# A graph network kernel: SyncE gathers ten blocks of layer two row by row, in place of GpSimd

## The reference

```python
def _sage_conv(x, src, dst, W_l, b_l, W_r):
    msgs = x[src]
    agg = jax.ops.segment_sum(msgs, dst, num_segments=N_NODES)
    deg = jax.ops.segment_sum(jnp.ones((src.shape[0],), x.dtype), dst, num_segments=N_NODES)
    mean = agg / jnp.maximum(deg, 1.0)[:, None]
    return mean @ W_l + b_l + x @ W_r
...
h = jax.nn.relu(_sage_conv(x, src, dst, W1_l, b1, W1_r))
h = jax.nn.relu(_sage_conv(h, src, dst, W2_l, b2, W2_r))
return h @ W3 + b3
...
x = _layernorm(x + _L0_gnn_ref(x, edge_index, ...), axis=-1)
```

## Time and profile before

| | us |
|---|---|
| median of 3 runs (lowest, highest) | 3304.33 (3302.39, 3308.82) |
| the profiled execution | 3299.5 |
| its span, first to last instruction | 3297.4 |
| PE busy, of the span | 2754.1 |
| POOL busy | 2379.8 |
| DVE busy | 1457.7 |
| ACT busy | 497.5 |

### The profile page before, as it was taken

One profiled execution on the slowest core, in us unless ns is written; L12 is line 12 of the kernel. 1 busy time (PEld: TensorE's weight loads), 2 busy tenths in 40 slices (PEclk: granted clock), 3 DMA queues, 4 the chain that ended last, 5 costly groups with the idle time before them and its releaser, 6 DMA issues.

```text
span 3297.4 us, 61445 instructions
## 1 busy us (share of the span) xinstructions
PE 2754.1 (84%) x13183; PEld 2294.5 (70%) x13184; DVE 1457.7 (44%) x3301; ACT 497.5 (15%) x1511; POOL 2379.8 (72%) x2439
## 2 busy tenths in 40 slices
PE   4788899899899899888866779878879879988876
PEld 3555687678678688677754567767768767767765
DVE  5676555555555555433323333333333333333332
ACT  2000110101111111111110112112112112212113
POOL 4765777677677677767747777777777777777775
PEclk7989999999999999999988889999999999999999
DMA  4443577577677777877655657757757757757743
GB/s 117 130 134 112 169 237 246 173 231 238 203 219 238 222 218 240 263 217 218 206 180 177 190 174 224 216 172 227 216 162 233 221 169 225 225 168 229 219 128 109
DMA packets 495816, 650.77 MB, mean 197 GB/s; under 512 B 184192, under 2 KB 414454, under 8 KB 492503
## 3 DMA queue, kind: packets, MB, share of 16 engines
q0 software_dynamic: 116736, 318.92, 32.6%
q1 hardware_dynamic: 298164, 253.95, 25.2%
q10 hardware_dynamic: 80800, 76.82, 7.7%
HBM read 579.07 MB, written 70.40 MB: 197 GB/s over the span
## 4 chain that ended last, share of the span: by engine, by line
PE 29%; POOL 24%; issue 18%; DVEq 14%; DMA 7%; DVE 7%; SPq 1%; ACT 1%; ACTq 0%; POOLq 0%; PEld 0%; PEldq 0%
POOL ring L420 24%; PE ps L507 16%; PE ps L578 5%; DMA ring<-z_rows,scol 4%; PE psY L622 3%; DVEq L917 2%; DVE oh L971 2%; PE psY L611 2%; DVEq L937 2%; DVE acc L907 1%; DMA counts<-scratch 1%; DVE oh L929 1%; PE psB L552 1%; DVEq L1067 1%; DVEq L914 1%
## 5 line engine op out<-in xcount | busy, mean ns | idle before, releaser
L507 PE MATMUL ps<-ring,oh 128*125 128x257 f32 (+1 forms) x6384 | 1586.9, 400 | 375.7 <-DMA ring<-z_rows,scol 203.6
L507 PEld LDWEIGHTS ps<-ring,oh 128*125 128x125 f32 x6384 | 1221.7, 196 | 649.5 <-issue 462.4
L420 POOL DMA_INDIRECT ring<-in_x,scol x1216 | 1193.4, 981 | 493.7 <-issue 349.8
L420 POOL DMA_INDIRECT ring<-z_rows,scol x1216 | 1185.8, 975 | 397.7 <-issue 355.5
L929 DVE SCALAR_TENSOR_TENSOR oh<-dcol,cf,iota 128x500 f32<-128x500 int16 x798 | 591.4, 741 | 609.9 <-issue 328.3
L907 DVE TENSOR_TENSOR acc<-ps,acc x802 | 338.8, 422 | 608.0 <-PE ps L507 415.4
L578 PE MATMUL ps<-scratch 128*125 128x257 f32 (+1 forms) x2000 | 481.2, 388 | 19.4 <-issue 13.4
L578 PEld LDWEIGHTS ps<-scratch 128*125 128x125 f32 x2000 | 456.1, 294 | 39.3 <-issue 21.5
L1268 ACT ACTIVATE work<-psT,b2c 128x125 f32<-128x125 f32 x200 | 62.0, 362 | 1196.2 <-PE psT L673 1196.2
L1232 ACT COPY work<-psY 125x256 f32<-125x256 f32 x100 | 37.2, 372 | 1306.1 <-PE psY L611 1306.1
L552 PE MATMUL psB<-oh 128*128 (+1 forms) x546 | 160.2, 391 | 81.7 <-DVE oh L971 80.7
(11 more groups left out here) (120 smaller groups left out, 1100.2 us busy)
## 6 DMA issues: line engine op xcount, KB each, us to landing
scratch<-counts SPq DMA_DIRECT2D x200, 312.5 KB
scratch<-in_x SPq DMA_DIRECT2D x114, 512.0 KB, 4.2
scratch<-z_rows SPq DMA_DIRECT2D x114, 512.0 KB, 4.0
counts<-scratch SPq DMA_DIRECT2D x25, 1250.0 KB
work<-in_x ACTq DMA_DIRECT2D x200, 125.0 KB
ring<-in_x,scol POOLq DMA_INDIRECT x1216
ring<-z_rows,scol POOLq DMA_INDIRECT x1216
scratch<-in_x SPq DMA_DIRECT2D x114, 128.0 KB, 5.2
```

What stands on the lines that cost most here:

```text
L420: pool.indirect_dma_start(ring[:, slot, b, 0:D], None, rows_dram, bass.IndirectOffsetOnAxis(scol[:, n - C0:n - C0 + 1], 0)).then_inc(rows[ ...
L507: mm = pe.matmul(psA[0:WN, bass.ds(bank, W)], oh[:, R if later else slot, b, :], ring[:, slot, b, 0:W], start=(b == 0), stop=(b == nb - 1))
```

## The change

In layer two, and there alone, two groups of each of the five stages get their first block from SyncE: the groups 27 and 47 of the stage (`own_group`), both in slot 3, behind the tenth and the twentieth dense step. The block lands in a place of its own behind the ring, `own`. GpSimd leaves out the first block of these ten groups (`lead`), so that it issues 1206 blocks in layer two where it issued 1216.

- SyncE loads the block's 128 addresses, straight from the input `src`, into one partition of `tables` (`load_picks`, two small DMAs for each stage). In the dense steps 2 to 9 and 11 to 18 of a stage, behind the three DMAs of `load_step`, it reads 16 of the addresses into registers (two loads of eight) and issues 16 DMAs of one row of 1 KB, whose source address is in a register (`own_rows`). That makes 128 DMAs for a block and 1280 in all. Before the second block's first rows it waits until TensorE has read the first one.
- In steps 9 and 19 SyncE waits until all 128 rows have landed and group 23 or 43 of the stage has been read, and then adds one to a new semaphore, `s_led` (`own_ready`).
- TensorE, ahead of the fourth group of each dense round in layer two, computes in registers whether this is an own group (`lead_row`), waits for `s_led` and takes the first block's operand from an address in a register. For the fourth slot it counts its semaphore in a register of its own, `turn3`, since only three blocks come from GpSimd there; this adds one register instruction to each round of layer one and to the other rounds of layer two.
- Some small tiles change their place, to make room.

```diff
+LEAD = (R - 1) * GB * RW
+def own_group(l, w, k):
+    return (40 if l else 4 + STAGE) + STAGE * w + 8 + 20 * k + 19
...
+            def own_rows(rows_dram, l, w, t):
+                m = w
+                k, s = (0, t - 2) if t < 10 else (1, t - 11)
+                if not 0 <= s < 8:
+                    return
+                if s == 0 and k == 0:
+                    sp.wait_ge(s_picks[m % 2], 32 * (m // 2 + 1))
+                if s == 0 and k == 1:
+                    sp.wait_ge(s_gr[l], own_group(l, w, 0) + 1)
+                elif s == 0 and w > 0:
+                    sp.wait_ge(s_gr[l], own_group(l, w - 1, 1) + 1)
+                for e in range(s * 16, s * 16 + 16, 8):
+                    sp.load(pick, picks[:, m % 2, k, e:e + 8])
+                    for j in range(8):
+                        sp.dma_start(own[e + j:e + j + 1, 0:D],
+                                     rows_dram[bass.ds(sp.snap(pick[j], min_val=0, max_val=N - 1), 1), :]).then_inc(
+                                         s_own[k], 16)
+            def own_ready(l, w, t):
+                if t not in (9, STEPS - 1):
+                    return
+                k = t // 10
+                sp.wait_ge(s_own[k], 16 * P * (w + 1))
+                sp.wait_ge(s_gr[l], own_group(l, w, k) - R + 1)
+                sp.sem_inc(s_led, 1)
...
                 for t in range(STEPS):
                     load_step(z_dram, w, t)
+                    if t == 2 and w + 1 < HW:
+                        load_picks(1, w + 1)
+                    own_rows(z_dram, 1, w, t)
+                    own_ready(1, w, t)
...
-                    for b in range(GB):
-                        if g >= R and b == 0:
+                    lead = int(l == 1 and g in own_groups(l))
+                    for b in range(lead, GB):
+                        if g >= R and b == lead:
                             pool.wait_ge(s_gr[l], g - R + 1)
...
+                    row = ring[:, slot, b, 0:W]
+                    if l == 1 and slot == R - 1 and b == 0:
+                        row = rows_flat[:, bass.ds(pe.snap(lead, min_val=LEAD, max_val=R * GB * RW), W)]
...
-                pe.wait_ge(rows[l][i], pe.snap(turn, min_val=16, max_val=16 * GB * NGG))
+                pe.wait_ge(rows[l][i], pe.snap(turn3 if i == R - 1 else turn, min_val=16, max_val=16 * GB * NGG))
...
+                def lead_row(j):
+                    pe.reg_alu(body, j, 205, ALU.mult)
...
+                    pe.reg_add(turn3, turn3, 48)
+                    pe.wait_ge(s_led, pe.snap(led, min_val=1, max_val=2 * HW + 1))
+                    pe.reg_alu(lead, lead, R * GB * RW - LEAD, ALU.mult)
+                    pe.reg_add(lead, lead, LEAD)
...
+                        if l == 1 and dense and i == R - 1:
+                            lead_row(j)
+                        elif i == R - 1:
+                            pe.reg_add(turn3, turn3, 16 * GB)
```

More of the change, by code:

```diff
@@ L78, in hot_end, with own_groups @@
     return 4 + STAGE * (w + 1) + STAGE
+LEAD = (R - 1) * GB * RW
+def own_group(l, w, k):
+    return (40 if l else 4 + STAGE) + STAGE * w + 8 + 20 * k + 19
+def own_groups(l):
+    return [own_group(l, w, k) for w in range(HW) for k in range(2)]
 def window_order():
@@ L156, in build @@
         acc = sb("acc", [P, (NW + 1) * RW])
-        ring = sb("ring", [P, R, GB, RW])
+        rows_all = sb("ring", [P, R * GB + 1, RW])
+        ring = rows_all[:, 0:R * GB, :].rearrange("p (r b) n -> p r b n", b=GB)
+        rows_flat = rows_all.rearrange("p q n -> p (q n)")
+        own = rows_all[:, R * GB, :]
         scol = sb("scol", [P, NC], I32)
@@ L230, in build @@
         k_i = k_u.bitcast(I32)
+        one = scratch[0:1, u:u + P]
+        u += P
         assert u <= 2 * JP * PW + 2 * SJ * (WN + RW)
@@ L251, in build @@
         rows = [[sem(f"rows{l}_{k}") for k in range(R)] for l in range(2)]
+        s_own = [sem(f"s_own{k}") for k in range(2)]
+        s_led = sem("s_led")
+        s_picks = [sem(f"s_picks{k}") for k in range(2)]
         s_oh = [sem(f"s_oh{l}") for l in range(2)]
@@ L392, in _ @@
                 sp.wait_ge(s_zd[q], 16 * (NW // 2))
+            give(sp, s_led)
+            load_picks(1, 0)
             fallback(z_dram, 0, STEPS)
@@ L401, in _ @@
             pool.memset(ed_i[:, 1, NT - 1, :], int(BIG)).then_inc(s_pad, 1)
-            pool.memset(ring[:, :, :, D:RW], 1.0).then_inc(s_ring1, 1)
+            pool.memset(rows_all[:, :, D:RW], 1.0).then_inc(s_ring1, 1)
             ready = 0
@@ L506, in pair @@
                 for b in range(nb):
+                    row = ring[:, slot, b, 0:W]
+                    if l == 1 and slot == R - 1 and b == 0:
+                        row = rows_flat[:, bass.ds(pe.snap(lead, min_val=LEAD, max_val=R * GB * RW), W)]
                     mm = pe.matmul(psA[0:WN, bass.ds(bank, W)], oh[:, R if later else slot, b, :],
-                                   ring[:, slot, b, 0:W], start=(b == 0), stop=(b == nb - 1))
+                                   row, start=(b == 0), stop=(b == nb - 1))
                     if b == nb - 2 and not later:
@@ L714, in four @@
                             fallback(l, general.index(i) % 2)
+                    if l == 1 and dense:
+                        pe.reg_mov(lead, LEAD)
                 if l == 0:
                     for i in range(4):
+                        if i == R - 1:
+                            pe.reg_add(turn3, turn3, 16 * GB)
                         one_group(i)
@@ L728, in layer @@
                             four(builds=True)
[L729 to L730 removed]
+                        with pe.Fori(0, STEPS // 2) as j:
+                            four(builds=True, dense=True, j=j)
                     with pe.Fori(0, 2):
                         four(general=(0, 1, 2, 3))
[L733 to L734 removed]
+                    with pe.Fori(0, STEPS // 2) as j:
+                        four(dense=True, j=j)
                 else:
@@ L740, in layer @@
                             four()
-                        with pe.Fori(0, STEPS // 2):
-                            four(dense=True)
+                        with pe.Fori(0, STEPS // 2) as j:
+                            four(dense=True, j=j)
                 with pe.Fori(0, STEPS // 4 + (1 if l else -2)):
```

35 lines of the change are left out of this document (26 added, 9 removed).

## The result

| | before | after |
|---|---|---|
| median of 7 runs (lowest, highest), us | 3303.17 (3299.98, 3308.82) | 3286.62 (3281.95, 3294.27) |
| ratio to before, 95% interval | | 0.9953 [0.9939, 0.9967] |
| the profiled execution, its span | 3299.5, 3297.4 | 3292.56, 3290.7 |
| layer one, GpSimd's first to last gather | 1679.7 | 1686.3 |
| layer two, GpSimd's first to last gather | 1556.0 | 1540.4 |

The change makes the kernel 0.47% faster, 15.5 us by the ratio. By the interval of the ratio the gain is anything from 10.9 to 20.1 us, so the size of the miss is read better from the length of layer two than from the medians.

The account below looks back on a forecast made before the run. GpSimd's issue of 1216 blocks was taken to bound layer two. Span 3297.4 - 12.5 (ten blocks) + 1.5 (layer one) = 3286.4 us; against the median 3304.3 - 11.0 = 3293.3 us, range 3288 to 3307.

Parts of the forecast that it names:

- The bound: Layer two: lasts exactly as long as GpSimd needs for its 1216 blocks, 1556 us, at 1.28 us each.
- The worth of a block: GpSimd, layer two: each block left out saves 1.25 to 1.28 us; ten blocks, 12.5 us taken.
- at most the mean: GpSimd, layer two: upper end of a block's worth, 1556/1216 = 1.28 us, as slow blocks may go on being slow.
- Layer one's 1.5 us: TensorE, layer one: one more register instruction in each of 76 rounds costs 1.5 us, bounds 0 and 3.2.
- SyncE's rows: SyncE's queue, layer two: 0.38 us a row, 8.8 us of a 10.2 us step; upper end 0.65 and 13.1 us.
- SyncE keeps up: SyncE's queue, dense steps with rows: at the lower end 8.8 us of issue fits in a step of 10.2 us.
- rival one: SyncE can't issue the rows in time and GpSimd stalls: about 3405 us at 0.7 us a row; chance 0.11.
- The wait for `s_led`: TensorE, tightest in stage 3 at step 9: the block is complete with 3 us to spare; price 0.
- TensorE's seven instructions: TensorE, before each fourth group in layer two's 50 dense rounds: 15 to 35 us, hidden beside waiting for rows; price 0.
- the ring's reserve: GpSimd's 16-block ring, layer two: TensorE may be late by an estimated 8 us before GpSimd stalls.
- Rival three: Layer two: one-row DMAs crowd one DMA engine; about 3420 us at 0.3 us a row; chance 0.07.

Follow-up runs that it names:

- g3: Changed kernel with GpSimd leaving out 50 blocks of layer two, gathered by nobody, no rows on SyncE: 3236.9 us, 0.9800 of before.
- h2: Changed kernel, but GpSimd also gathers the ten blocks and TensorE reads GpSimd's copy: 3303.6 us, 0.9998 of before.
- h3: Changed kernel with register loads added on SyncE that were dropped when built, so the changed kernel again: 3288.0 us, 0.9956 of before.
- k1: Changed kernel with eight of each step's 16 rows fetched in two halves, on a chip with pausing queues: 4324.4 us, 1.1081 of before.
- h1: Changed kernel with the ten blocks gathered by nobody, no rows on SyncE, TensorE's wait kept: 3285.0 us, 0.9946 of before.
- e1: Changed kernel, unedited, on a chip whose queues paused: 4138.3 us, 1.0427 of before.

## Why the prediction was wrong, and where it was right

**The bound was read rightly.** The one pause of 0.305 us before every gather, whatever it is put down to, said that GpSimd sets layer two alone, against the busy shares of the earlier trace rows. Leaving out 50 blocks gave 70 us (g3), and the rows alone gave nothing (h2).

**The worth of a block was the term that was mis-sized.** The prediction took 1.25 us and named 1.28 as the upper end. Measured in layer two: 1.41 in g3, and for ten blocks 15.8 us or 1.58 each, from the means of two executions (1557.3) and of five (1541.4). The step that failed is "at most the mean": the slow gathers were taken to stay or to go in proportion, and they went faster than that, 3.3 us in place of 0.3 for ten blocks (8.0 in place of 1.5 in g3). The upper end was an average over gathers and not a bound. Why they went faster stays open.

**Layer one's 1.5 us** didn't show. With layer two at 15.8 us less and nothing for layer one the gain would be 15.8 us, with the upper bound of 3.2 it would be 12.6. The ratios of the changed kernel in three series (0.9953, 0.9961, and 0.9956 in h3) are gains of 15.5, 12.9 and 14.5 us and leave room for 0 to 3.

**The range.** Its lower end was built from 12.8 us and the spread of three runs, and then set at 3288. An unexplained part of a duration should have widened it: those 35 us of excess stood in the earlier trace rows as the gap between median and maximum. The median of before moved by 1.2 us as well, from three runs to seven.

**SyncE's rows: hidden, but not because SyncE keeps up.** A row takes 0.42 to 0.44 us and not 0.38, since a second register instruction of 29 ns goes with it, and a load of eight registers takes 0.77 us on SyncE's queue where TensorE's took 0.595:

```profile
L398 SPq TENSOR_LOAD <-tables x160: 686/770/2561, 1981.7 to 3126.5; - x160
```

The step is 10.5 us instead of 8.8, against the 10.2 counted for TensorE. The DMA itself was sized well (0.228, for 0.254 from the earlier trace rows). So "SyncE keeps up" failed, in the prediction's own terms: (10.5 - 2.7)/16 is 0.49 us for a row, everything included, past the 0.47 from which it falls behind and short of the 0.54 from which GpSimd was to stall. It does fall behind, by up to 8.2 us, and the price of nothing came out right because the loads' two steps of lead and the ring took it. That was nearer to rival one than the text had it, and to that extent the right direction was luck. The mechanism of that rival, its waiters included, is what happened on the pausing chips; its price there, 4% of the time, was sized right in order (115 us at 0.7 us a row; 177 us at 0.80), but the form of the arithmetic was wrong, as k1 showed.

**The wait for `s_led`, and TensorE's seven instructions.** The 3 us to spare aren't there. At the first block of stages 0 and 2 of the changed kernel TensorE comes first and waits: its seven instructions take 1.39 and 2.58 us there, the wait in them, against 0.84 in the median. In stage 3, the place that the prediction worked out, SyncE is 1.0 us ahead. Outside the waits the seven take 0.84 us each round, 42 us in all, over the 15 to 35 written. None of it reaches GpSimd, whose pauses stay 0.305 us, so the price of 0 holds by the ring's reserve. h1, which has the seven instructions and SyncE 11 to 19 us ahead at all ten places, has a layer two shorter by 0.9 us than h3 in its series, and equal to that of the changed kernel's first profile.

**Rival three** isn't seen. The landings of SyncE's loads are 3.9/4.4/5.7 us after 3.7/4.4/5.1. SyncE's queue has 2580 packets more than in the earlier trace rows, for 1290 DMAs more (1280 rows and ten of addresses):

```profile
q1 hardware_dynamic: 300744, 255.27, 25.3%
```

That is two packets for each, as the 32 a step of the prediction assume, and so a row isn't spread over the 16 engines. This much of the rule cited there from the Trainium skill ("DMA: Bandwidth & Descriptors", section "Why a DMA increments its semaphore by 16 and not by 1") the trace bears out; whether it is always the lowest-numbered engine no view shows. It changed nothing.

## What to carry to other kernels

An engine with one and the same pause before every instruction, whatever the trace puts it down to, is the bound of its stretch, and taking instructions off it pays one for one. Work moved to an idle queue is free only while that queue's lag fits into the lead of its loads; past that point each microsecond is paid at every step, so the reserve belongs into the sum and the margin should survive a slower queue: here steps of 10.5 us against a consumer's 10.4 gave 0.5% on some chips, and steps of 15.4 to 15.7 us took 4% on others. Whether a queue keeps up is seen in when its loads start: at once when a place comes free, or later. When a duration has a tail over its median, bound the worth of an instruction with the tail's full share and not with the mean.

## What the runs showed of the hardware

- SyncE issues a DMA of one row of 1 KB with its source address in a register in 0.228 us (median of 1280), like one of 256 bytes with a fixed address (0.233 and 0.254 us, one of each), and a new one every 0.42 us (median) with the two register instructions ahead of it. Each adds two packets to its queue.
- A register load of eight values took 0.77 us on SyncE's queue and 0.595 us on TensorE's.
- GpSimd's indirect DMA of 128 rows takes 946 ns, and over 1 us in 31% of those during which VectorE begins the add of line 907 out of PSUM, against 3% of the others, and in none of 32 during which it begins only the equally long add of line 1028.
- The same program took 3304 us on some chips and 3902 to 3969 us on others. On the latter, in e1, 730 instructions of SyncE start 650 to 800 ns after the one before them, against 84 in the profile of the changed kernel, and 747 start within 25 ns of it, against none, where the shortest step was otherwise longer. What causes these pauses, and whether they would be there without the recording of a profile, no run here tells.
